# Reordering one step of an LSTM: a quarter of half 1's first matmuls ahead of half 0's second ones, and the seed copies behind the gates

## The reference

```python
xz = einsum('ntd,dk->ntk', x, Wx) + b          # all tokens at once
def step(carry, xz_t):                         # 256 times, one after the other
    prev_h, prev_c = carry
    z = xz_t + prev_h @ Wh                     # 16x256 by 256x1024
    ai, af, ao, ag = split(z, 4, axis=1)
    next_c = sigmoid(af)*prev_c + sigmoid(ai)*tanh(ag)
    next_h = sigmoid(ao) * tanh(next_c)
x = x + lstm(x)
mid = gelu(x @ base_down + (x @ a2) @ b2.T)    # a1, b1, a2, b2: 256x8 for each sequence
x = x + mid @ base_up.T + (mid @ b1) @ a1.T
```

## Time and profile before

| | us |
|---|---|
| median of 3 runs (lowest, highest) | 621.93 (621.92, 622.44) |
| span of the profiled execution, first to last instruction | 618.6 |
| PE busy, PEld busy | 600.8, 444.2 |
| DVE busy, ACT busy | 471.6, 386.8 |

### The profile page before, as it was taken

The page is one execution under the profiler, slowest core; times in us unless marked ns, Lnnn a source line. Parts: engine busy times, 40 slices in busy tenths (PEclk is TensorE's granted clock), DMA queues, the critical chain, the costliest instruction groups (busy, mean ns, idle before and its releaser), DMA issues.

```text
span 618.6 us, 33951 instructions
## 1 busy us (share of the span) xinstructions
PE 600.8 (97%) x14120; PEld 444.2 (72%) x14120; DVE 471.6 (76%) x2543; ACT 386.8 (63%) x2158; POOL 38.6 (6%) x77
## 2 busy tenths in 40 slices
PE   8689998999999999999999999999999999999997
PEld 5565556777777777777777777777777777777886
DVE  3576667778888888788888888888878888888772
ACT  2365656666666666666666666666666666666662
POOL 3000000000000000000000000000000000000000
PEclk9899999999999999999999999999999999999999
DMA  5993630232333123333321232332122323211201
GB/s 162 233 217 141 181 45 13 38 46 55 55 55 53 32 33 49 54 55 54 56 34 32 47 54 55 54 55 41 38 33 55 55 55 55 44 37 24 54 21 36
DMA packets 31499, 38.74 MB, mean 63 GB/s; under 512 B 3632, under 2 KB 29536, under 8 KB 30321
## 3 DMA queue, kind: packets, MB, share of 16 engines
q1 hardware_dynamic: 31282, 36.51, 30.5%
q0 software_dynamic: 64, 0.07, 0.1%
HBM read 15.59 MB, written 4.19 MB: 32 GB/s over the span
## 4 chain that ended last, share of the span: by engine, by line
PE 95%; DVE 1%; issue 1%; DMA 1%; SPq 0%; ACT 0%; ACTq 0%
PE z L698 36%; PE x_bank L496 18%; PE z_o L698 9%; PE aux L522 8%; PE out_bank L545 7%; PE out_bank L627 3%; PE aux L507 3%; PE aux L474 2%; PE out_bank L577 2%; PE aux L529 2%; PE out_bank L566 1%; PE x_bank L566 1%; DMA seed<-proj 1%; PE x_bank L522 1%; DMA x_nat<-in_x 0%
## 5 line engine op out<-in xcount | busy, mean ns | idle before, releaser
L698 PEld LDWEIGHTS z<-wh,h_t 128*16 128x16 f32 x8160 | 159.8, 96 | 116.8 <-DVE h_t L855 87.1
L698 PE MATMUL z<-wh,h_t 128*16 128x96 f32 x8160 | 233.5, 248 | 4.9 <-issue 2.1
L835 DVE STREAM_TRANSPOSE z<-z 128x96 f32<-128x96 f32 x512 | 151.4, 298 | 86.7 <-PE z L698 67.9
L413 ACT ACTIVATE gates<-z 128x48 f32<-128x48 f32 x512 | 107.7, 210 | 156.9 <-DVE z L835 129.3
L496 PE MATMUL x_bank<-wx,x_t 128*128 128x256 f32 x512 | 156.0, 392 | 0.5 <-ACT x_t L331 0.5
L337 ACT ACTIVATE z<-seed 128x96 f32<-128x96 f32 x512 | 123.7, 242 | 5.8 <-DMA seed<-proj 5.8
L698 PE MATMUL z_o<-wh,h_t 128*16 128x64 f32 x4080 | 106.1, 219 | 0.8 <-issue 0.8
L845 DVE SCALAR_TENSOR_TENSOR prod<-gates 128x32 f32<-128x32 f32 x512 | 97.7, 191 | 0.6
L850 DVE SCALAR_TENSOR_TENSOR gates<-prod 128x16 f32<-128x16 f32 x512 | 84.2, 165 | 8.7
L496 PEld LDWEIGHTS x_bank<-wx,x_t 128*128 128x128 f32 x512 | 80.6, 195 | 6.4 <-issue 1.5
L698 PEld LDWEIGHTS z_o<-wh,h_t 128*16 128x16 f32 x4080 | 81.2, 97 | 1.4 <-issue 1.3
(11 more groups left out here) (114 smaller groups left out, 439.0 us busy)
## 6 DMA issues: line engine op xcount, KB each, us to landing
seed<-proj SPq DMA_DIRECT2D x128, 128.0 KB
w<-in_L_cond_W SPq DMA_DIRECT2D x4, 2048.0 KB, 10.2
x_nat<-in_x SPq DMA_DIRECT2D x32, 128.0 KB, 4.2
out<-y_nat SPq DMA_DIRECT2D x32, 128.0 KB, 4.2
wx<-in_L_cond_Wx SPq DMA_DIRECT2D x2, 512.0 KB, 5.9
wh<-in_L_cond_Wh SPq DMA_DIRECT2D x2, 256.0 KB, 7.1
wh<-in_L_cond_Wh SPq DMA_DIRECT2D x1, 512.0 KB, 6.5
w<-in_L_cond_W SPq DMA_DIRECT2D x1, 256.0 KB, 4.5
```

The source lines that it names most:

```text
L413: act.activation(gates[s % 2][m][:, 0:3 * B].rearrange("p (g b) -> p g b", b=B), zt[m].rearrange("p (g c) -> p g c", c=C)[:, :, 0:B], ACT. ...
L698: ins = pe.matmul(dst, h_prev[:, kc, :], rhs, start=False, stop=(kc == 1), skip_group_check=True)
L835: dve.transpose(zt[m], z_bank[m][:, 0:GC]).then_inc(turned[m], 1)
```

## The change

Two things move. On PE, the product of the first half of h with half 1's g gate (32 of its 96 columns) is put ahead of the wait for the second half of h; its other 64 columns (i and f) stay behind half 0's second product. The loop over `order` becomes calls of a function `recur`. On ACT, the copy of a half's next seed comes right after that half's gates, where it stood around the second tanh of the cell; its own wait on the gates goes (ACT has just done them), and the wait for the next block's seed transfer moves to the head of the block's last step.

```diff
+                    if s == TB - 1 and more:
+                        act.wait_ge(seed_loaded[ahead.par], (ahead.turn + 1) * (16 * NQ))
                     gates_of(0)
+                    if more:
+                        seed_bank(ahead.par, s_next, 0)
                     gates_of(1)
+                    if more:
+                        seed_bank(ahead.par, s_next, 1)
                     tanh_o()
                     tanh_cell(0)
-                    if more:
-                        act.wait_ge(gates_ready[0], n)
-                        seed_bank(ahead.par, s_next, 0)
                     tanh_cell(1)
                     if more:
-                        act.wait_ge(gates_ready[1], n)
-                        seed_bank(ahead.par, s_next, 1)
                         act.wait_ge(ht_ready[1], n + 1)
                         seed_o(ahead.par, s_next)
-                    if s == TB - 2 and (front or k.p == 0):
-                        ahead = k.plus(1)
-                        act.wait_ge(seed_loaded[ahead.par], (ahead.turn + 1) * (16 * NQ))
...
-                    order = ((0, 0), (1, 0), (0, 1), (1, 1), (0, OG), (1, OG))
-                    for i, (kc, m) in enumerate(order):
-                        if kc not in [other[0] for other in order[:i]]:
-                            pe.wait_ge(ht_ready[kc], n)
-                        if kc == 0:
-                            pe.wait_ge(seeded_o if m == OG else seeded[m], n)
+                    def recur(kc, m, first=0, count=G - 1, done=None):
...
-                                dst = z_bank[m][rows, 0:GC].rearrange("p (g c) -> p g c", c=C)
-                                rhs = gates_of[:, 0:G - 1, unit:unit + C]
+                                dst = z_bank[m][rows, C * first:C * (first + count)].rearrange("p (g c) -> p g c", c=C)
+                                rhs = gates_of[:, first:first + count, unit:unit + C]
...
+                    pe.wait_ge(ht_ready[0], n)
+                    pe.wait_ge(seeded[0], n)
+                    recur(0, 0)
+                    pe.wait_ge(seeded[1], n)
+                    recur(0, 1, 2, 1)
+                    pe.wait_ge(ht_ready[1], n)
+                    recur(1, 0, done=z_ready[0])
+                    recur(0, 1, 0, 2)
+                    recur(1, 1, done=z_ready[1])
+                    pe.wait_ge(seeded_o, n)
+                    recur(0, OG)
+                    recur(1, OG, done=zo_ready)
```

More of the change, by code:

```diff
@@ L695, in one_block @@
                                 unit = m * P + C * j
-                                dst = z_bank[m][rows, 0:GC].rearrange("p (g c) -> p g c", c=C)
-                                rhs = gates_of[:, 0:G - 1, unit:unit + C]
+                                dst = z_bank[m][rows, C * first:C * (first + count)].rearrange("p (g c) -> p g c", c=C)
+                                rhs = gates_of[:, first:first + count, unit:unit + C]
                             ins = pe.matmul(dst, h_prev[:, kc, :], rhs, start=False, stop=(kc == 1),
                                             skip_group_check=True)
-                        if kc == 1:
-                            ins.then_inc(zo_ready if m == OG else z_ready[m], 1)
+                        if done:
+                            ins.then_inc(done, 1)
+                    pe.wait_ge(ht_ready[0], n)
[10 more added lines that the diff above has]
+                    recur(1, OG, done=zo_ready)
                     if done and done.seq.exists():
```

## The result

The changed kernel is slower: 626.69 us median (623.70 to 628.78, 11 runs) against 621.93 (620.36 to 623.29, 11 runs), a ratio of 1.0076 with a 95% interval of 1.0054 to 1.0098. I had forecast 618.1, with a range up to 625.0. Its profiled execution took 623.7 us, of which 621.9 are the span, so 1.8 us lie around a span; by that the profiled execution of before (618.6) was at about 620.4, the low end of its runs, and the one of after at the low end of its own. The two traces differ by 3.3 us, the medians by 4.8.

What follows compares the result with a forecast made beforehand. A loop of latencies bounds the kernel: 216 steps gain 0.02, 4.3 us, less 0.5 for instructions, 3.8 off the profiled 618.6, 614.8; the median lies 3.3 above: 618.1. Range 615.5 to 625.

Steps and rivals of the forecast that it cites:

- What bounds the kernel: Each step goes round a loop of latencies through PE, DVE and ACT, 2.219 us a step, despite PE's 97% busy.
- the tie at products 1: On DVE, products 1 wait equally for the queue and gates 1; earlier gates 1 would gain about 0.01 us.
- the two ties: Products 1 (DVE's queue and gates 1) and the second tanh (cell 1 and the seed copy) each have two equally late inputs.
- The small passes: On PE, two 32-column g gate passes, 0.028 us each, fit before h1's product with 0.01 to 0.04 to spare.
- the hole: PE's gap between the first product's passes and the second product's loads, 0.06 us, to take the two g passes.
- the rival of a late start: If PE's start 0.11 behind h0 is a first load's price, not the seed's, no gain: 622.4 us; chance 0.18.
- that of dear small passes: Between h0's and h1's products, 32-column passes cost as much as 64-column ones: 625.4 us; chance 0.18.
- PE's other work is no obstacle: PE's last other piece before the step starts at 306.19, and all of it can start 0.05 us sooner.
- The gain of the copies: On ACT, the second tanh starts 0.48 instead of 0.50 behind cell 0; 0.02 us a step, including the tie's 0.01.
- The moved wait for the seed transfer stays ahead of the same gates: On ACT, the moved wait leaves behind it only what stood there before; no cost was counted.
- More instructions: On PE, 4,096 more instructions on 28,240, 14.5%, cost 0 to 1.3 us; 0.5 taken.

Runs made afterwards that it cites:

- the ACT half alone: Kernel before with only the ACT part of the change (seed copies behind the gates, wait at the block's last step), PE as before: 618.01 us, ratio 0.9940.
- the PE half alone: Kernel before with only the PE part of the change (early g gate columns), ACT order as before: 660.8 us, ratio 1.0621.
- 4.5 fetches a block: Changed kernel with, in addition, the o gate's first product in eight matmuls, another 4,096 PE instructions: 654.38 us, ratio 1.0521.
- spread transfers: Kernel before with the o gate's product in eight matmuls and a block's four seed transfers spread over five steps: 629.76 us, ratio 1.0133.
- the number of instructions alone: Kernel before with the o gate's first-half product in eight matmuls of 32 columns instead of four of 64: 654.60 us, ratio 1.0504.

## Why the prediction was wrong

*What bounds the kernel, and the tie at products 1: right.* The loop goes round latencies; with products 1 freed of gates 1, cell 1 came 0.27 behind cell 0. Products 1 start no earlier for it (0.05 behind cell 0 in both traces), but they last 0.182 instead of 0.192 us, since they no longer wait for an input. Each half of the change by itself leaves one of the two ties in place: with the ACT half alone cell 1 stays at 0.28, with the PE half alone the copy holds the tanh at 0.50. Both are needed for a step of 2.20.

*The small passes: right.* They fit into the hole. h0 ends at 307.99 in the step above and the first load starts at 308.05, 0.06 behind it instead of 0.08:

```profile
308.05 0.30 PEld L692 LDWEIGHTS z<-wh,h_t 128*16 128x16 f32 x16 [0.40 <-DVE h_t L862]
```

and 16 loads, those of the first product and of the early g gate, are through in 0.30. In the middle steps of the blocks (medians from the starts of the records) the first matmul follows h0 by 0.056 instead of 0.11, the two passes of the g gate start 0.028 apart, as worked out, and the second product starts 0.23 behind the start of h1, as before. So both the rival of a late start and that of dear small passes are out. The reason I gave was the seed, and the halves confirm it: with the seed late the step grew by 0.02, and in the ACT half alone the first matmul follows h0 by 0.055 in those steps in which PE is free by then. "PE's other work is no obstacle" was wrong for one step in eight: in the second step of a block the first product follows close on a matmul of L494 and starts 0.11 behind h0, z0 comes 0.013 later, and the step stays at 2.21.

*The gain of the copies: 0.01 too much.* I gave the move of the copies 0.01 beside the 0.01 of the tie, and it brought nothing of its own. The start of the second tanh moved by 0.017, of which 0.011 are the earlier cell 1. Only some 0.008 come from the copy: from the end of cell 1 to the tanh it is 0.034 without the copy ahead of it and was 0.042 with it, a difference that the rounded rows (0.05 against 0.03) made 0.02. And that is lost again, because an instruction that waits for its input on an idle engine lasts longer than one queued behind another: 0.187 against 0.180. The trace of before had shown the like, in products 1, 0.19 long when they waited and 0.18 in the block's first step, where they did not:

```profile
303.70 0.18 DVE L845 SCALAR_TENSOR_TENSOR prod<-gates 128x32 f32<-128x32 f32 x1
```

*"The moved wait for the seed transfer stays ahead of the same gates": wrong.* I counted its order and not what a second wait on an instruction costs. It is 0.06 us in the last step of 25 blocks, 1.5 us, and takes back what the other steps of the block gain. Before, the same wait mostly came ahead of other ACT work at the end of step 6, which hid it. The trace of before had a price: the block's first step, in which DVE's first turn carries one wait more, is longer by 0.07 (17.75 for eight steps, of which seven of 2.21 leave 2.28). There PE's last record for z0 starts 0.34 behind h1, as in the other steps, and the second semaphore had reached its value a block earlier.

*"More instructions": this step failed, and decided the sign.* I took the waits for issue of before, let them grow with the number of instructions, and got 0 to 1.3 us. But what a longer stream costs is not in proportion: 4,096 instructions cost 33 us on the kernel before, and next to nothing when the seed transfers are small. In the change they cost 3.3 us of stalls in the traced execution (7.4 against 4.1), the whole difference between the two traces. A fetch of 256 instructions competes with those transfers; when it comes late, PE runs dry, for 1.3 and 1.6 us in the two stalls shown. The row that should have stopped me is the DMA share of single steps, which I didn't read: in the kernel before, too, it is about 1 (packets overlap, so it can pass 1) in two steps of a block:

```profile
304.36:306.57 2.21, 2.21 (x55) 1.65 (x55) 1.76 (x11) 1.37 (x9) 0.00 (x0) 1.00 0.96 149
306.57:308.78 2.21, 2.21 (x55) 1.64 (x55) 1.90 (x11) 1.37 (x9) 0.00 (x0) 1.00 1.15 158
```

The Trainium skill, "Runtime: NRT & Kernel Launch", section "Instruction fetch mechanics", gives the 256 instructions, which the packets bear out, and calls the cost of crossing such a boundary mostly hidden. For most fetches that holds here too; the stalls behind full DMA engines contradict it.

In sum: the traced span of after is 621.9 where the forecast had 614.8. Of these 7.1 us the stalls are 2.8 (3.3 against the 0.5 that I took), the halved gain of the steps some 2.2 (0.01 in 216 steps), the wait 1.5; 0.6 I can't place, nor why after's median execution is 3.0 us longer than its traced one. The steps of the change give 0.06 us a block if the wait is left where it was (17.69 against 17.75), 1.7 us in 28 blocks; the moved wait takes that back; and the instruction supply adds the loss. Shown by one change each: the transfers (small or spread), the number of instructions, the wait. Open: why the stalls cost over 30 us with the late seed copies or with 4.5 fetches a block, and so little in the changed kernel with the same number of instructions; what holds a fetch up (its packet is seen to start late and behind full engines, not why); why PE goes on only some 1.4 us after the packet's end; the stalls whose packet came late with the engines idle; and what remains of the 33 us with spread transfers (8 us).

## What to carry to other kernels

An instruction added to a long unrolled stream can cost through the engine's DMA fetch too: before splitting a matmul to fill a hole, look at the DMA share step by step, and spread large transfers so that no step is full. A wait that is moved should be moved onto an instruction that isn't on the path, even if what it waits for is long done. And where a chain has two ties in a row, look at both: removing one of them alone did not shorten the step here.

## What the runs showed of the hardware

Four matmuls that go to different column groups start 7 ns apart, and the next four follow 0.028 (32 columns), 0.056 (64) or 0.083 us (96) behind them (medians from after's trace). A second wait on an instruction cost 0.06 us on ACT and 0.07 on DVE here, though it had long been fulfilled. An instruction that waits for its input on an idle engine lasts 0.007 (ACT) to 0.01 (DVE) longer than the same one queued behind another. And an instruction fetch that starts late behind a saturated DMA can leave PE without instructions for 1 to 2 us; in the traces of after and of the number of instructions alone it went on 1.3 to 1.7 us after the packet's end. Over a whole kernel such stalls cost up to 33 us of 655.
